# Reordering the query stage of a six-layer transformer kernel: key products half a turn later, folds spread over both halves

## The chip, the cores and the metric

The kernel runs on one core of a Trainium2 chip. A core has five engines with their own instruction streams, which wait for each other on semaphores: TensorE (PE in the rows; its weight loads are PEld), VectorE (DVE), ScalarE (ACT), GpSimd (POOL) and SyncE (SP), which here issues every DMA. The metric is the device time of one execution in microseconds (us); lower is better.

## The reference

The program is six residual layers over x, 16 samples of 64 tokens with 256 channels: a cross attention with low-rank keys, a self attention, a feed-forward layer, a second cross attention, a gated delta-rule layer and a mixture of experts. The change touches the first half of the first one, whose queries are

```
q_hk  = (hidden_q @ Wq.T).reshape(Bv, Sv, H, K)          # H = 16 heads, K = 128
q_big = jnp.einsum('bshk,hkq->bshq', q_hk, w_kc_q)       # q: 192
q_big = _apply_rope(q_big, sin_q, cos_q)
q_r   = jnp.einsum('bshq,hqr->bhsr', q_big, W_qr)
k_r   = jnp.einsum('bld,hdr->bhlr', kv_r, W_kr)
scores = jnp.einsum('bhsr,bhlr->bhsl', q_r, k_r)
```

The kernel folds the weight matrices first (Wq with w_kc_q, W_qr with W_kr), so that a head costs one product of the 1024 normalized tokens with a 256 x 192 matrix, the rotation, and one product with a 192 x 64 matrix.

## The kernel before

The program has four phases; the change lies in `phase1` (lines 154 to 497), the query stage. It works on pairs of heads in eight turns (`u` = 0 to 7, `PAIRS0`), and the 1024 tokens are split into two halves (`f` = 0, 1) of 512. The order of work is written out by hand, for each engine a list of calls in its block:

- **TensorE.** `fold(h)` (L278) multiplies the weights of head h into PSUM bank 0, two matmuls with 192 columns. `fold_pair(u)` (L288) does the small weight products of the pair into bank 1. `queries(u, f)` (L300) multiplies one half of the tokens with the folded weights `cw`: three banks `t` = 0, 1, 2 (2 to 4 for half 0, 5 to 7 for half 1), two matmuls each, which the trace records as 12 instructions of 512 columns. `keys(u, f)` (L313) multiplies the rotated queries `rot` with `mw`, 12 matmuls (24 records) that overwrite the first two banks of that half. `turn(t)` transposes one tile of tokens.
- **ScalarE.** `folded(h)` (L353) moves bank 0 into `cw`, `swap(u, f)` (L363) copies the third bank with its quarters exchanged into `sw` (four instructions), `keep_keys(u, f)` (L373) moves the key products into `tts`.
- **VectorE.** `rope(u, f)` (L430) is the rotation, nine operations of 512 columns; it reads the three banks, `sw` and tables, and leaves `rot`. The additions at L442, L444 and L449 read SBUF alone. `latent` and `butterfly` are side work of the turns 1 to 6, for later layers.
- **GpSimd.** Two multiplications of the weights `ug` by a scale (L405), as soon as their 2 MB have landed, and one of `dn` (L407).
- **SyncE.** `load(h)` (L190) fetches one head's weights: `wk` (384 KB) and `wr` (64 KB), double-buffered, and waits before it until `fold_pair` has released the buffer (`wf`). `store(u, f)` (L197) writes `tts` to DRAM. `ahead(u)` (L214) fetches weights of later layers, among them the 2 MB `ug` in turn 2. Everything goes through one queue in program order.

What each waits for: `queries(u, 0)` for `cw` of both heads (`cs`), `queries(u, f)` from turn 1 on for `keep_keys(u-1, f)` (`ts0`, `ts1`), since the key products lie in its banks; `fold(h)` for ScalarE to have moved the fold before (`cs`); `keys(u, f)` for the rotation (`rope0`, `rope1`). TensorE's loop:

```
for u in range(PAIRS0):
    queries(u, 0)
...
    queries(u, 1)
    if u + 1 < PAIRS0:
        fold(2 * u + 2)
    keys(u, 0)
    if u + 1 < PAIRS0:
        fold(2 * u + 3)
        fold_pair(u + 1)
    keys(u, 1)
```

After the last turn SyncE reads the stored queries back (`load_queries`, L203), once all of half 0 has landed, and only then stores the last half 1; then all engines meet at a barrier.

Of the kernel before, what the change touches and what calls it, by code (L numbers as in the profile page):

```python
# [7 lines left out]
ACT = mybir.ActivationFunctionType  # L8
# [3 lines left out]
B, S, D = 16, 64, 256  # L12
TILES = B * S // P
DC = D // P
L, DCTX = 128, 64
# [138 lines left out]
def phase1(nc, d, sb, semaphores, C, over, X, HT, PS, con, carrier, bn, mv, ve, rstd, hn, kvr, kvT, ctT, TTd, W2, weights, early, b1, q):  # L154
# [4 lines left out]
    with ExitStack() as ctx:  # L159
# [27 lines left out]
        with nc.Block() as block:  # L187
            @block.sync
            def _(sp):
                def load(h):  # L190
                    if h > 1:
                        sp.wait_ge(s["wf"], h // 2)
                    sp.dma_start(wk[:, h % 2, :], d["l0x_k"][h:h + 1, :, :].rearrange("a p n -> (a p) n")).then_inc(s[f"w{h % 2}"], 16)
                    sp.dma_start(wr[64 * (h % 2):64 * (h % 2) + R0, h // 2 % 2, :], d["l0x_r"][h:h + 1, :, :].rearrange("a p n -> (a p) n")).then_inc(s[f"w{h % 2}"], 16)

# [59 lines left out]
                load(3)  # L255
                for u in range(PAIRS0):
                    ahead(u)
                    store(u, 0)
                    if u + 2 < PAIRS0:
                        load(2 * u + 4)  # L260
                        load(2 * u + 5)
                    if u == PAIRS0 - 1:
                        sp.wait_ge(s["ctt"], 16)
                        sp.wait_ge(s["next"], 14 * 16)
                        load_queries()
                    store(u, 1)

            @block.tensor
            def _(pe):
# [16 lines left out]
                    mm.then_inc(s["cf"], 1)  # L286

                def fold_pair(u):  # L288
                    if u > 0:
                        pe.wait_ge(s["ws"], u)  # L290
                    for t in range(3):
                        for r in range(2):
                            rows = slice(64 * r, 64 * r + R0)
                            mm = pe.matmul(PS[rows, 1, t * DCTX:(t + 1) * DCTX], wr[rows, u % 2, t * 64:(t + 1) * 64], wr[rows, u % 2, CQ:RW],
                                           start=True, stop=True)
                    for r in range(2):
                        mm = pe.matmul(PS[64 * r:64 * r + DCTX, 1, D:2 * D], wk[:, r, D + CQ:D + CQ + DCTX],
                                       wk[:, r, D + CQ + DCTX:KW], start=True, stop=True)
                    mm.then_inc(s["wf"], 1)

                def queries(u, f):
                    if f == 0:
                        pe.wait_ge(s["cs"], u * 2 + 2)
                    if u == 0:
                        pe.wait_ge(s["hT"], 4 * f + 4)
                    else:
                        pe.wait_ge(s[f"ts{f}"], u)
                    for t in range(3):
                        for k in range(DC):
                            mm = pe.matmul(PS[:, qbank(f, t), :], cw[:, u % 2, k, t * P:(t + 1) * P],  # L310
                                           HT[:, k, f * 512:(f + 1) * 512], start=(k == 0), stop=(k == DC - 1))
                    mm.then_inc(s[f"q{f}"], 1)
# [19 lines left out]
                for u in range(PAIRS0):  # L332
                    queries(u, 0)
                    if u == 0:
                        for t in range(4, 8):
                            turn(t)
                    queries(u, 1)
                    if u + 1 < PAIRS0:
                        fold(2 * u + 2)
                    keys(u, 0)  # L340
                    if u + 1 < PAIRS0:
                        fold(2 * u + 3)
                        fold_pair(u + 1)
                    keys(u, 1)

            @block.scalar
            def _(a):
# [5 lines left out]
                def folded(h):  # L353
# [1 line left out]
                    a.wait_ge(s["cf"], h + 1)  # L355
                    a.activation(cw[:, u % 2, :, :].rearrange("p k (t r n) -> p k t r n", t=3, r=2)[:, :, :, p, :],
                                 PS[:, 0, 0:DC * CQ].rearrange("p (k t n) -> p k t n", k=DC, t=3), ACT.Copy).then_inc(s["cs"], 1)
                    if p == 1:
                        a.wait_ge(s["wf"], u + 1)
                        a.activation(mw[:, u % 2, :, :], PS[:, 1, 0:3 * DCTX].rearrange("p (t n) -> p t n", t=3), ACT.Copy).then_inc(s["ms"], 1)  # L360
                        a.activation(W2[:, u, :], PS[:, 1, D:2 * D], ACT.Copy).then_inc(s["ws"], 1)

                def swap(u, f):  # L363

# [16 lines left out]
                    keep_hT(t)  # L381
                folded(0)
                folded(1)
                for u in range(PAIRS0):
                    if u == 0:
                        for t in range(4, 8):
                            keep_hT(t)
                    swap(u, 0)
                    swap(u, 1)
                    if u + 1 < PAIRS0:  # L390
                        folded(2 * u + 2)
                    keep_keys(u, 0)
                    if u + 1 < PAIRS0:
                        folded(2 * u + 3)
                    keep_keys(u, 1)

            @block.gpsimd
            def _(g):
# [11 lines left out]
            def _(v):  # L410
# [79 lines left out]
                v.wait_ge(s["cons"], 16)  # L490
                for u in range(PAIRS0):
                    rope(u, 0)
                    rope(u, 1)
                    if 1 <= u <= 6:
                        latent(u - 1)
                    if 4 <= u <= 6:
                        butterfly(u - 4)

# [1954 lines left out]
```

## Time and profile before

| | |
|---|---|
| median of 3 runs | 1542.12 us (1539.15 to 1542.85) |
| the profiled execution | 1550.27 us |
| its span, first to last instruction | 1548.2 us |
| TensorE busy | 1408.3 us (91%) |
| VectorE busy | 1104.5 us (71%) |
| ScalarE, GpSimd busy | 602.0 us, 607.7 us (39% each) |
| the query stage's turns | 17.5 to 174 us of the span |
| in 17.4 to 182 us: TensorE, VectorE, ScalarE busy | 132.0, 111.8, 59.4 us of 164.6 |

The busy time of TensorE counts a matmul from its start to its modelled end, so overlapping ones add up to more than the engine's real occupation; where this text speaks of how long TensorE is taken, it goes by the distance between starts. In a row of the timeline the first number is the start, the second the time to the end of the merged group, and the bracket says how long the engine was idle before and whose result ended that.

### The profile page before, as it was taken

What the parts mean: (1) busy time and instruction counts of PE and PEld (TensorE: products, weight loads), DVE (VectorE), ACT (ScalarE), POOL (GpSimd) and SP (SyncE); (2) the same over time, 40 slices, a digit from 0 to 9 for tenths busy, and PEclk for the clock granted to TensorE, in tenths of its full rate; (3) what the DMA queues carried; (4) which work ended last, traced back from release to release, by engine and by line L of the source; (5) the groups of instructions that cost most, each with busy time, mean ns of one, the idle gap of its engine ahead of it and who ended that gap; (6) DMA issues with size and microseconds to landing.
All of it is one profiled execution on the core that took longest, in us unless ns stands there. A gap on an engine that the chain in (4) does not pass through costs nothing. (4 is left out here: it accounts for less than half of the span.)

```text
span 1548.2 us, 32593 instructions
## 1 busy us (share of the span) xinstructions
PE 1408.3 (91%) x13504; PEld 974.7 (63%) x13504; DVE 1104.5 (71%) x1710; ACT 602.0 (39%) x1012; POOL 607.7 (39%) x935
## 2 busy tenths in 40 slices
PE   6788689999997878999999999999999878999999
PEld 3344368877885445667766666776667665655556
DVE  5768486588557777998898988889999735534443
ACT  3333254345324533554445555445445421111110
POOL 1200143244314646567656657665657610000000
PEclk9999899999998999999999999999999988999999
DMA  8534300110000131121222121222122105000000
GB/s 227 178 89 112 75 1 1 28 28 2 1 1 1 31 78 37 42 58 42 55 52 46 40 58 43 55 51 51 48 44 51 34 18 218 0 1 0 14 1 14
DMA packets 125955, 74.63 MB, mean 48 GB/s; under 512 B 95536, under 2 KB 107056, under 8 KB 124016
## 3 DMA queue, kind: packets, MB, share of 16 engines
q1 hardware_dynamic: 125808, 72.55, 17.9%
q8 instruction: 107, 1.75, 0.5%
q14 instruction: 40, 0.33, 0.1%
HBM read 54.68 MB, written 17.83 MB: 47 GB/s over the span
## 5 line engine op out<-in xcount | busy, mean ns | idle before, releaser
L1877 DVE SCALAR_TENSOR_TENSOR W<-PS,wc,W 128x504 f32<-128x504 f32 x375 | 271.0, 732 | 31.6 <-ACT W L1570 21.9
L1570 ACT ACTIVATE W<-PS,wc 128x512 f32<-128x512 f32 x125 | 85.9, 687 | 154.0 <-PE PS L1273 94.9
L2207 PE MATMUL PS<-HT,wgu 128*128 128x512 f32 x320 | 143.5, 592 | 0.0
L1273 PE MATMUL PS<-HT,wv 128*128 128x512 f32 x252 | 120.2, 608 | 6.8 <-DVE W L1877 6.8
L2341 DVE SCALAR_TENSOR_TENSOR act<-th,PS 128x512 f32<-128x512 f32 x48 | 33.0, 687 | 128.8 <-ACT th L2267 128.8
L1458 PE MATMUL PS<-wo,ogT 128*128 128x256 f32 x512 | 117.2, 388 | 7.6 <-DVE dl L1948 5.1
L1273 PE MATMUL PS<-HT,wkq 128*128 128x512 f32 x248 | 118.1, 620 | 2.9 <-DVE W L1877 2.9
L1296 PE MATMUL PS<-wz,HT 128*128 128x256 f32 x512 | 120.0, 386 | 0.0
L1458 PEld LDWEIGHTS PS<-wo,ogT 128*128 128x128 f32 x512 | 99.3, 195 | 22.2 <-DVE dl L1948 5.3
L2267 ACT ACTIVATE th<-PS 128x512 f32<-128x512 f32 x48 | 28.7, 597 | 206.4 <-PE PS L2207 206.4
L1296 PEld LDWEIGHTS PS<-wz,HT 128*128 128x128 f32 x512 | 94.6, 191 | 17.4 <-issue 4.0
L1777 POOL TENSOR_TENSOR rr<-nm,con 128x8 f32<-128x8 f32 x16 | 31.9, 1994 | 182.7 <-DVE nm L1908 182.7
L1574 ACT ACTIVATE W<-W 128x512 f32<-128x512 f32 x125 | 78.5, 628 | 61.3 <-DVE W L1877 59.7
L2207 PEld LDWEIGHTS PS<-HT,wgu 128*128 128x128 f32 x320 | 60.6, 190 | 60.2 <-issue 58.4
L1808 POOL TENSOR_TENSOR tm<-sy,ti 128x15 f32<-128x15 f32 (+7 forms) x240 | 69.8, 291 | 55.4 <-DMA sy<-a_rows 37.9
L2219 PE MATMUL PS<-wd,act 128*128 128x256 f32 x384 | 89.8, 379 | 0.0
L2219 PEld LDWEIGHTS PS<-wd,act 128*128 128x128 f32 x384 | 72.7, 190 | 26.4 <-issue 18.6
L310 PE MATMUL PS<-HT,cw 128*128 128x512 f32 x192 | 86.7, 607 | 0.5 <-ACT HT L350 0.5
L1273 PEld LDWEIGHTS PS<-HT,wkq 128*128 128x128 f32 x248 | 47.9, 199 | 57.3 <-issue 49.7
L1810 POOL TENSOR_TENSOR ti<-ti,tm 128x15 f32<-128x15 f32 (+7 forms) x240 | 71.6, 298 | 18.8
L1273 PEld LDWEIGHTS PS<-HT,wv 128*128 128x128 f32 x252 | 44.0, 189 | 50.0 <-issue 45.9
L1888 DVE SCALAR_TENSOR_TENSOR yB<-W 128x512 f32<-128x512 f32 x64 | 62.2, 973 | 6.7 <-ACT W L1574 5.4
(277 smaller groups left out, 2938.1 us busy)
## 6 DMA issues: line engine op xcount, KB each, us to landing
a_rows<-AT SPq DMA_DIRECT2D x16, 512.0 KB, 3.1
wk<-in_l0x_k SPq DMA_DIRECT2D x16, 384.0 KB, 3.9
wgu<-in_moe_gu SPq DMA_DIRECT2D x5, 1024.0 KB, 16.4
queries_scratch<-tts SPq DMA_DIRECT2D x32, 128.0 KB, 2.8
wkq<-in_gdn_w SPq DMA_DIRECT2D x16, 256.0 KB, 3.1
wv<-in_gdn_w SPq DMA_DIRECT2D x16, 256.0 KB, 2.9
wz<-in_gdn_w SPq DMA_DIRECT2D x16, 256.0 KB, 2.7
wo<-in_gdn_w SPq DMA_DIRECT2D x16, 256.0 KB, 2.9
```

Source lines behind the costliest of these rows:

```text
L310: mm = pe.matmul(PS[:, qbank(f, t), :], cw[:, u % 2, k, t * P:(t + 1) * P], HT[:, k, f * 512:(f + 1) * 512], start=(k == 0), stop=(k == DC ...
L1273: mm = pe.matmul(PS[:, qbank(h, q), :], w[:, o:o + DK], HT[:, k, f * 512:(f + 1) * 512], start=(k == 0), stop=(k == DC - 1))
L1296: mm = pe.matmul(PS[:, zbank(j, m), w * 256:(w + 1) * 256], HT[:, k, n * P:(n + 1) * P], wz[:, k * 2 * DK:(k + 1) * 2 * DK], start=(k == 0 ...
L1458: mm = pe.matmul(PS[:, wbank(m), w * D:(w + 1) * D], ogT[:, hv, n * P:(n + 1) * P], wo[:, hv, :], start=(hv == 0), stop=(hv == 1))
L1570: a.activation(acc[:, flows(h, q), :], PS[:, qbank(h, q), :], ACT.Copy, scale=wc[:, h % 2, 4 * c + 3:4 * c + 4]).then_inc(s["tap"], 1)
L1574: a.activation(th[:, flows(h, q), :], acc[:, flows(h, q), :], ACT.Tanh, scale=0.5).then_inc(s["th"], 1)
L1808: g.tensor_tensor(t, each(sy[:, c, c + 1:SUB], m), over(ti[:, 0, c, 0:m], n), ALU.mult).then_inc(s["sub"], 1)
L1810: g.tensor_tensor(ti[:, 0, c + 1:SUB, 0:m], ti[:, 0, c + 1:SUB, 0:m], t, ALU.subtract).then_inc(s["sub"], 1)
L1877: v.scalar_tensor_tensor(a0, p0, wc[:, h % 2, 4 * c + 2 - k:4 * c + 3 - k], a0, ALU.mult, ALU.add).then_inc(s["conv"], 1)
L1888: v.scalar_tensor_tensor((yA, yB)[f][:, c, :], th[:, k, :], 1.0, acc[:, k, :], ALU.add, ALU.mult).then_inc(s["y"], 1)
L2207: mm = pe.matmul(PS[:, 2 * (i % 2) + w, :], pack[:, k, w, :], HT[:, k, f * N:(f + 1) * N], start=(k == 0), stop=(k == DC - 1))
L2219: mm = pe.matmul(acc(t)[:, 0:D], act[:, i % RING, t * P:(t + 1) * P], wd[:, m, :], start=(m == 0), stop=(m == MC - 1))
```

## The change

TensorE's loop gets another order, and ScalarE's with it. The two folds of the next pair no longer follow `queries(u, 1)` together: `fold(2u+2)` and `fold_pair(u+1)` come behind `queries(u, 0)`, `fold(2u+3)` behind `queries(u, 1)`. `keys(u, 1)` is done in the next turn, between the two query halves; `keys(u, 0)` stays in its turn, behind `queries(u, 1)` and the fold. The banks inside `queries` are filled in the order 2, 0, 1, and the wait for `keep_keys` comes only before bank 0. `load(h)` also waits for the fold that used the buffer (`cf`), `fold_pair` also for the second weights (`w1`), `store(u, 0)` goes behind the two loads in SyncE's queue, and on VectorE `latent` stands between the two rotations.

```diff
@@ sync @@
                     if h > 1:
                         sp.wait_ge(s["wf"], h // 2)
+                        sp.wait_ge(s["cf"], h - 1)
...
                 for u in range(PAIRS0):
                     ahead(u)
-                    store(u, 0)
                     if u + 2 < PAIRS0:
                         load(2 * u + 4)
                         load(2 * u + 5)
+                    store(u, 0)
@@ tensor @@
                 def fold_pair(u):
+                    pe.wait_ge(s["w1"], u * 32 + 32)
...
                     if u == 0:
                         pe.wait_ge(s["hT"], 4 * f + 4)
-                    else:
-                        pe.wait_ge(s[f"ts{f}"], u)
-                    for t in range(3):
+                    for t in (2, 0, 1):
+                        if u > 0 and t == 0:
+                            pe.wait_ge(s[f"ts{f}"], u)
...
+                    if u + 1 < PAIRS0:
+                        fold(2 * u + 2)
+                        fold_pair(u + 1)
+                    if u > 0:
+                        keys(u - 1, 1)
                     queries(u, 1)
                     if u + 1 < PAIRS0:
-                        fold(2 * u + 2)
+                        fold(2 * u + 3)
                     keys(u, 0)
-                    if u + 1 < PAIRS0:
-                        fold(2 * u + 3)
-                        fold_pair(u + 1)
-                    keys(u, 1)
+                keys(PAIRS0 - 1, 1)
@@ scalar @@
                     swap(u, 0)
+                    if u + 1 < PAIRS0:
+                        folded(2 * u + 2)
+                    if u > 0:
+                        keep_keys(u - 1, 1)
+                    if u + 1 < PAIRS0:
+                        folded_pair(u + 1)
                     swap(u, 1)
                     if u + 1 < PAIRS0:
-                        folded(2 * u + 2)
+                        folded(2 * u + 3)
                     keep_keys(u, 0)
-                    if u + 1 < PAIRS0:
-                        folded(2 * u + 3)
-                    keep_keys(u, 1)
+                keep_keys(PAIRS0 - 1, 1)
@@ vector @@
                     rope(u, 0)
-                    rope(u, 1)
                     if 1 <= u <= 6:
                         latent(u - 1)
+                    rope(u, 1)
```

`folded_pair(u)` is the second half of the old `folded`, the moves of bank 1 into `mw` and `W2`. In the order of instructions TensorE's turn 1 reads before (L310 are the queries, L284 a fold, L294 and L297 the pair's products, L322 the key products):

```order
L310 MATMUL PS<-HT,cw 128x512 x12
L284 MATMUL PS<-wk 128x192 x2
L322 MATMUL PS<-rot,mw 64x256 x12
L284 MATMUL PS<-wk 128x192 x2
L294 MATMUL PS<-wr 64x64 x6
L297 MATMUL PS<-wk 64x256 x2
L322 MATMUL PS<-rot,mw 64x256 x12
```

and in the changed kernel:

```order
L312 MATMUL PS<-HT,cw 128x512 x6
L285 MATMUL PS<-wk 128x192 x2
L296 MATMUL PS<-wr 64x64 x6
L299 MATMUL PS<-wk 64x256 x2
L324 MATMUL PS<-rot,mw 64x256 x12
L312 MATMUL PS<-HT,cw 128x512 x6
L285 MATMUL PS<-wk 128x192 x2
L324 MATMUL PS<-rot,mw 64x256 x12
```

The same instructions stand in the turn; the queries are now cut in two, and each half is followed by a fold and by key products, of which the first (the upper L324) are those of the turn before. In turn 0 there are no such products, and after turn 7 one set is left over.

SyncE's queue around the 2 MB transfer of turn 2 reads before

```order
L223 DMA ug<-in_ffn_ug 128x4096
L200 DMA queries_scratch<-tts 64x4x128 x2
L193 DMA wk<-in_l0x_k 128x768
L194 DMA wr<-in_l0x_r 64x256
```

and in the changed kernel

```order
L201 DMA queries_scratch<-tts 64x4x128 x4
L224 DMA ug<-in_ffn_ug 128x4096
L194 DMA wk<-in_l0x_k 128x768
L195 DMA wr<-in_l0x_r 64x256
```

(`ug`, `wk` and `wr` are weights, `queries_scratch` is the DRAM copy of the queries). The stores of half 0 no longer stand between the 2 MB and the next weights; the first load follows at once.

## Rows read from the trace of the kernel before

**Rows 1.** The page's first line: length of the profiled span

```profile
span 1548.2 us, 32593 instructions
```

**Rows 2.** Waits from 17 to 185 us, longest in total first: us, times, longest

```profile
PE PS L322 <- DVE rot L449: 17.6, 9, 7.3
PE PS L284 <- ACT cw L356: 6.4, 7, 1.0
```

**Rows 3.** Timeline, TensorE, one turn: start us, us, engine, line, op, xcount, [idle before]

```profile
38.24 10.57 PE L310 MATMUL PS<-HT,cw 128*128 128x512 f32 x24
48.65 0.81 PE L284 MATMUL PS<-wk 128*128 128x192 f32 x4
49.45 1.53 PE L322 MATMUL PS<-rot,mw 64*64 64x256 f32 x24
51.89 0.89 PE L284 MATMUL PS<-wk 128*128 128x192 f32 x4 [0.91 <-ACT cw L356]
53.20 0.65 PE L297 MATMUL PS<-wk 128*64 128x256 f32 x4
54.88 1.53 PE L322 MATMUL PS<-rot,mw 64*64 64x256 f32 x24 [1.02 <-DVE rot L449]
56.34 4.13 PE L310 MATMUL PS<-HT,cw 128*128 128x512 f32 x9
```

**Rows 4.** Timeline, ScalarE, the same turn

```profile
43.70 2.38 ACT L370 ACTIVATE sw<-PS 32x512 f32<-32x512 f32 x4 [4.72 <-PE PS L310]
48.84 2.38 ACT L370 ACTIVATE sw<-PS 32x512 f32<-32x512 f32 x4 [2.77 <-PE PS L310]
51.26 0.49 ACT L356 ACTIVATE cw<-PS 128x384 f32<-128x384 f32 x1
51.64 0.59 ACT L377 ACTIVATE tts<-PS 128x512 f32<-128x512 f32 x1
```

**Rows 5.** Timeline, VectorE, the same turn

```profile
43.70 0.69 DVE L437 TENSOR_TENSOR ra<-PS,con 128x512 f32<-128x512 f32 x1 [6.96 <-PE PS L310]
54.74 2.28 DVE L454 TENSOR_TENSOR kvT<-b,con 128x2048 f32<-128x2048 f32 x1
```

**Rows 6.** Timeline around the stall in turn 2, all engines

```profile
58.42 0.60 SPq L223 DMA_DIRECT2D ug<-in_ffn_ug  x1
67.26 9.43 POOL L405 TENSOR_TENSOR ug<-ug,b 128x2048 f32<-128x2048 f32 x2 [52.28 <-DMA ug<-in_ffn_ug]
72.26 4.98 DVE L444 TENSOR_TENSOR rot<-rc,rd 128x512 f32<-128x512 f32 x1
79.22 2.84 PE L322 MATMUL PS<-rot,mw 64*64 64x256 f32 x24 [7.27 <-DVE rot L449]
81.99 3.42 PE L310 MATMUL PS<-HT,cw 128*128 128x512 f32 x5
88.45 1.79 ACT L370 ACTIVATE sw<-PS 32x512 f32<-32x512 f32 x3 [5.73 <-PE PS L310]
```

**Rows 7.** Timeline of turn 0: SyncE's queue, then TensorE between the halves

```profile
19.10 1.63 SPq L194 DMA_DIRECT2D wr<-in_l0x_r  x1
21.40 0.47 SPq L194 DMA_DIRECT2D wr<-in_l0x_r  x1
24.51 0.68 PE L275 MATMUL PS<-con,hn 128*128 128x128 f32 x4 [0.35 <-ACT HT L350]
25.66 1.55 PE L310 MATMUL PS<-HT,cw 128*128 128x512 f32 x3 [0.47 <-ACT HT L350]
```

**Rows 8.** DMA issues from 19 to 20 us, then 21.3 to 21.8: us to landing

```profile
wr<-in_l0x_r SPq DMA_DIRECT2D x1, 64.0 KB, 9.2
wr<-in_l0x_r SPq DMA_DIRECT2D x1, 64.0 KB, 8.2
```

**Rows 9.** Timeline, TensorE, the last key products

```profile
172.02 2.13 PE L322 MATMUL PS<-rot,mw 64*64 64x256 f32 x24 [3.90 <-DVE rot L449]
```

**Rows 10.** Windows, 173 to 174 us: busy by engine, granted clock, DMA share, GB/s

```profile
173.00:174.00 1.00, 1.00 (x12) 0.27 (x4) 0.00 (x0) 0.00 (x0) 0.00 (x0) 0.50 0.42 59
```

More of the change, by code:

```diff
@@ L357, in folded, with folded_pair @@
                                  PS[:, 0, 0:DC * CQ].rearrange("p (k t n) -> p k t n", k=DC, t=3), ACT.Copy).then_inc(s["cs"], 1)
[L358 to L361, printed above, removed]
+                def folded_pair(u):
+                    a.wait_ge(s["wf"], u + 1)
+                    a.activation(mw[:, u % 2, :, :], PS[:, 1, 0:3 * DCTX].rearrange("p (t n) -> p t n", t=3), ACT.Copy).then_inc(s["ms"], 1)
+                    a.activation(W2[:, u, :], PS[:, 1, D:2 * D], ACT.Copy).then_inc(s["ws"], 1)
                 def swap(u, f):
@@ L383, in _ @@
                 folded(1)
+                folded_pair(0)
                 for u in range(PAIRS0):
```

## Prediction

> **What bounds the kernel now.** I read the timeline of the query stage first, engine by engine, since a change of order can only move waits. The rows give one undisturbed turn, turn 1, from 38.24 to 56.34 us, so 18.10 us long [rows 3]. TensorE's own work in it, by distances between starts: 24 query records 10.41 us (48.65 less 38.24), a fold 0.80 (49.45 less 48.65), twice 1.60, a set of key products 1.46 (56.34 less 54.88), twice 2.92, and the pair's products at most 1.16 (from 51.89 + 0.80 to the end of the last at 53.20 + 0.65). That is 16.09 us; the other 2.0 are two gaps, 0.91 us for the fold's bank, which ScalarE moves only after its swap, and 1.02 us for VectorE's last addition [rows 3]. VectorE's two rotations take 11.04 us (54.74 less 43.70) with 2.28 of side work behind them [rows 5]. So TensorE is the bound in a plain turn, with two avoidable gaps.
>
> The waits by engine, the second view, name the same two for the whole stage: 17.6 us for the rotation and 6.4 us for `cw` [rows 2]. But 7.3 of the 17.6 are one wait. The timeline around it: the 2 MB of `ug` are issued at 58.42 and land at 67.26; GpSimd then multiplies for 9.43 us; in that time a VectorE addition of two SBUF tiles lasts 4.98 us, where the whole rotation is 5.52; TensorE idles 7.27 us and goes on at 79.22, and turn 3 starts at 81.99 instead of 74.4 [rows 6]. And it goes on slowly: the key products take 2.77 us (81.99 less 79.22) instead of 1.46, the first query half 6.46 us to its swap (88.45 less 81.99) instead of 5.46 (43.70 less 38.24) [rows 3, 4, 6]. That is TensorE at its lower level, 1.2 GHz; the tail shows the same after 3.90 us idle, 24 products in 2.13 us and a granted clock of 0.50 [rows 9, 10].
>
> **The plain turn after the change.** No instruction is added or removed on any engine in a turn. TensorE's chain, from the start of `queries(u, 0)`: first half 5.27 us (43.70 less 0.19 less 38.24; the swap starts 0.19 after the next TensorE work, 48.84 against 48.65), fold 0.80, pair 1.16, key products of the turn before 1.46, second half 5.14. Call this point F, 13.83 us in. Fold and key products take 2.26 more. The rotation of half 0 started at 5.46 and lasts 5.52, so it is done at 11.0, well before F + 0.80: the gap of 1.02 us is gone. The other gap only moves. The next queries need both halves of `cw`, and ScalarE moves the second behind its swap: before, the swap started at 48.84, the move at 51.26 and TensorE at 51.89, which is F + 3.24 [rows 3, 4]. So TensorE waits 3.24 - 2.26 = 0.98 us. The turn is 13.83 + 3.24 = 17.07; cutting the queries in two may show one weight load that was hidden, nothing to 0.2 us, and I take 17.1. **Each plain turn gains 1.0 us.**
>
> The other order of banks costs nothing and avoids a loss: ScalarE ends `keep_keys` at F + 0.19 + 2.42 + 0.38 + 0.59 = F + 3.6 [rows 4], and bank 0 is now wanted at F + 3.24 plus four records, 1.7 us; wanted first, it would have been 0.4 late. `keys(u, 1)` waits for a rotation that started at F + 0.19 and ended at F + 5.7; it is wanted at F + 10.5. Even with `latent` between the rotations (2.28 us, done at 13.3, half 1 ready at 14.0) VectorE keeps up.
>
> **Turn by turn**, against the profiled execution:
>
> - Turns 1, 3, 4, 5, 6: 5 x 1.0 = 5.0 us gained.
> - Turn 2: it lasted 81.99 - 56.34 = 25.65 us. In the new order `ug` is issued behind the store of `keys(1, 1)`, about 10.7 us into turn 2, and lands 8.84 later, 2.5 us into turn 3. GpSimd holds 2.5 to 11.9. The rotation of turn 2's half 1 ends at 2.4; that of turn 3's half 0 starts at 5.46, meets its first addition at 7.9, waits to 11.9 and ends at 15.0. Its key products are wanted at 14.6, and the 0.98 us wait follows anyway. The next rotation runs 17.3 to 22.8 and is wanted at 24.3. So this stall is hidden: 25.65 - 17.1 = 8.55 gained, and 1.0 for the slow clock in turn 3. What it costs without that cover is between 0 and what it cost before, 6.25 us and the clock.
> - Turn 0: here it gets worse. `fold(2)` and `fold_pair(1)` now stand before `queries(0, 1)`, which ran at 25.66. Their weights are behind the context tensors in the queue: issued 19.10 and 21.40, landing after 9.2 and 8.2 us, at 28.3 and 29.6 [rows 7, 8]. TensorE is free at 25.2 (24.51 + 0.68) and idles 3.1 us; the half starts at 29.6 + 1.16 = 30.8, 5.1 later. From there to turn 1 it was 12.58 us (38.24 less 25.66) and is 5.14 + 3.24 = 8.38, as one set of key products is left out and both gaps are less. Net 0.9 us lost.
> - The clock in turn 0: 3.1 us idle lies between the 1.02 us, after which the turn ran on at full rate, and 3.90 us, after which it did not [rows 3, 9]. Bounds 0 and 2.3 us (1.3 + 1.0 from the stall above); I take 1.1, the middle, as the row at 3.90 is the nearer.
> - Turn 7: one more set of key products before the last query half, 1.46 + 0.1: 1.6 lost. Behind the last half both programs are the same: the last swap, `keep_keys`, the read back.
> - Weights: `load(8)` now follows the 2 MB at once. At 2 MB in 8.84 us its 448 KB land 1.9 us behind them, 21.5 us into turn 2, wanted at 22.4; `load(9)` at about 23.4, wanted at 23.2. Between 0 and 1 us late, I take 0.3. The other moves in SyncE's queue have some microseconds of room: a store is awaited only a turn later.
>
> Sum: 5.0 + 8.55 + 1.0 - 0.9 - 1.1 - 1.6 - 0.3 = **10.7 us less**. The profiled execution took 1550.3 us with a span of 1548.2 [rows 1], 8 us above the median of the runs shown; the rows of the stage are waits set by order, which the other runs have too, so I take the difference off the median: 1542.1 - 10.7 = **1531.4 us**. Its own range is 1529 to 1535.
>
> **What the skill adds.** On the idle time in turn 0 the Trainium skill (TensorE: Matmul & The Clock Gate, section "Why this matters for your kernels") warns of idle gaps between bursts of matmuls, since the clock falls to its lower level in one. By it the full 2.3 us would be due and the result 1532.6 instead of 1531.4; the row at 3.90 us agrees with it, the rows show nothing at 3.1.
>
> The Trainium skill (SBUF — State Buffer, section "SBUF: two separate sides") has GpSimd and a VectorE operation with two SBUF inputs exclude each other for a whole instruction, whoever starts first. The 4.98 us addition agrees; where the 2 MB land in the new order decides who is held, which is the first rival.
>
> **Rivals.**
>
> 1. **The stall of turn 2 returns in turn 3.** GpSimd's 9.43 us still fall on the rotations. If the 2 MB land 3 or 4 us later than I have them (the weights behind them share the DMA engines), both multiplications can catch an addition each, and the key products wait. For it: 15.0 against 14.6 has no room. Against: every rotation now has some 4 us before it is wanted. Whole, it gives back 6.25 + 2.3: 1540; half of it 1535.5. Chance 0.08 and 0.10.
> 2. **Slower: the second weights arrive late in every turn.** `load(2u+5)` now waits for `fold(2u+3)`, is issued about 14.7 us into the turn, and `fold_pair` wants it at 17.1 + 6.1, 8.5 us later; before, both loads could go at 53.85 and were wanted from 66.75 on, 12.9 later (56.34 + 10.41) [rows 3]. It decides from a landing time of 8.5 us. In turn 0 such loads took 9.2 and 8.2 us [rows 8]. For a loss of over 0.3% each of six turns would have to wait 2.6 us, a landing of 11 us: with the idle time the clock would fall too, and the result would be 1548. Against it: the 9.2 us were behind over 3 MB. Chance 0.04.
> 3. **It goes better:** turn 0's weights land before they are wanted and no slow clock follows, or the 0.98 us wait is shorter: 10.7 + 1.1 + 0.3 and up to 3 more, 1527. Chance 0.08.
> 4. **The change does not do what it says:** the gap of 1.02 only joins the other one, as TensorE waits for `cw` longer (the move then comes behind something else in ScalarE's order). Turns stay at 18.1, the rest holds: 5 + 1 less gained, 1537.4. Chance 0.06; a small remainder, 0.04, I leave for no change.
>
> **The numbers.** The forecast has 0.60. A measurement can tell about 0.3%, 4.6 us, from no change. Faster by more than that, below 1537.5: the forecast, half of rival 1, rivals 3 and 4, 0.60 + 0.10 + 0.08 + 0.06 = 0.84, and 0.02 of the edge of rival 1. Within: the rest of it and the remainder, 0.10. Slower: 0.04. Range: from rival 3 to rival 1's whole price, 1527 to 1539, which leaves out rival 2, half of the whole of rival 1 and the ends.
>
> **What would show it.** In the profile after, a plain turn of 17.1 us with one wait of 0.9 to 1.0 us before `queries(u, 0)`, for `cw`, and none for the rotation until the last turn; no wait of over 1.5 us in turns 2 and 3, though a VectorE addition of 4 us; in turn 0 a wait of 3 us before the third fold and `queries(0, 1)` at about 30.8; turn 7 starting near 143 us (40.2 + 6 x 17.1 + 0.3). Wrong would be: a wait for the rotation in turn 3, turns above 17.5 us, or a wait for weights in every turn.

## The result and the profile after

The changed kernel takes 1535.47 us, median of 14 runs (1530.4 to 1539.67), beside 1542.59 us for the kernel before (14 runs, 1538.02 to 1547.27). The two medians differ by 7.1 us; the ratio is 0.9948, with a 95% interval of 0.9935 to 0.9960, which makes it 8.0 us faster, between 6.2 and 10.0. The forecast was 1531.4 with a range of 1527 to 1539, and faster; its own narrower range, 1529 to 1535, is missed by 0.5 us. The profiled execution took 1532.53 us. Of all the executions told of below, one ran in a slower state (1853.50 us at a mean granted clock of 0.745 instead of 0.97, the kernel with turn 0 in the old order) and is in no ratio.

The page's first lines, length of the span and TensorE's busy time:

```profile
span 1530.5 us, 32607 instructions
PE 1409.0 (92%) x13504; PEld 972.7 (64%) x13504; DVE 1097.3 (72%) x1710; ACT 601.7 (39%) x1012; POOL 608.7 (40%) x935
```

The span is 17.7 us below that of before [rows 1], much more than the runs differ. So the span can't be the measure; the stage that was changed has to be read by itself. Its waits, the view that answers to [rows 2] (us in total, times, longest):

```profile
PE PS L312 <- ACT cw L360: 6.0, 7, 0.9
PE PS L324 <- DVE rot L459: 4.5, 2, 3.9
PE PS L285 <- DMA wr<-in_l0x_r: 3.4, 1, 3.4
```

The wait for the rotation was 17.6 us and is 4.5, 3.9 of it the last key products, where it stood before as well [rows 9]. The wait for ScalarE's `cw` is still there, 6.0 for 6.4 us, now ahead of the queries. New is a wait of 3.4 us for weights.

TensorE's timeline of turn 1, the answer to [rows 3] (start, us, line, [idle before]; L312 are the queries, L285 a fold, L296 and L299 the pair's products, L324 the key products):

```profile
42.09 5.42 PE L312 MATMUL PS<-HT,cw 128*128 128x512 f32 x12 [0.89 <-ACT cw L360]
47.34 0.81 PE L285 MATMUL PS<-wk 128*128 128x192 f32 x4
48.09 0.56 PE L296 MATMUL PS<-wr 64*64 64x64 f32 x12
48.58 0.65 PE L299 MATMUL PS<-wk 128*64 128x256 f32 x4
49.17 1.53 PE L324 MATMUL PS<-rot,mw 64*64 64x256 f32 x24
50.62 5.42 PE L312 MATMUL PS<-HT,cw 128*128 128x512 f32 x12
55.88 0.81 PE L285 MATMUL PS<-wk 128*128 128x192 f32 x4
56.62 1.53 PE L324 MATMUL PS<-rot,mw 64*64 64x256 f32 x24
59.03 5.42 PE L312 MATMUL PS<-HT,cw 128*128 128x512 f32 x12 [0.89 <-ACT cw L360]
```

The turn lasts 59.03 - 42.09 = 16.94 us, where it was 18.10. One gap is left, 0.89 us for `cw`; the key products at 49.17 (those of turn 0) and at 56.62 start without one.

Turn 0, the same view, from the last token transposes to the fold behind the query half:

```profile
24.20 0.68 PE L276 MATMUL PS<-con,hn 128*128 128x128 f32 x4 [0.35 <-ACT HT L354]
28.30 1.17 PE L285 MATMUL PS<-wk 128*128 128x192 f32 x4 [3.41 <-DMA wr<-in_l0x_r]
29.88 0.91 PE L296 MATMUL PS<-wr 64*64 64x64 f32 x12 [0.41 <-DMA wr<-in_l0x_r]
31.77 7.33 PE L312 MATMUL PS<-HT,cw 128*128 128x512 f32 x12
38.93 0.81 PE L285 MATMUL PS<-wk 128*128 128x192 f32 x4
```

and the busy times and granted clock (third number from the right) in one microsecond of it:

```profile
29.00:30.00 1.00, 0.59 (x4) 0.12 (x4) 0.74 (x2) 0.49 (x1) 0.00 (x0) 0.50 1.06 379
```

TensorE is free at 24.9, waits 3.4 us for the first weights and 0.4 us for the second, and starts the half at 31.77. By then it runs at its lower level, 1.2 GHz: the half takes 38.93 - 31.77 = 7.16 us instead of the 5.26 of the same half in turn 1 (55.88 - 50.62).

The 2 MB of `ug` and what they release, answering to [rows 6]: SyncE's queue, GpSimd, VectorE's longest addition, TensorE's key products of turn 3 and the next queries.

```profile
69.60 0.61 SPq L224 DMA_DIRECT2D ug<-in_ffn_ug  x1
78.37 9.12 POOL L415 TENSOR_TENSOR ug<-ug,b 128x2048 f32<-128x2048 f32 x2 [63.37 <-DMA ug<-in_ffn_ug]
83.83 4.21 DVE L452 TENSOR_TENSOR rot<-ra,rb 128x512 f32<-128x512 f32 x1
90.72 1.53 PE L324 MATMUL PS<-rot,mw 64*64 64x256 f32 x24
92.92 5.42 PE L312 MATMUL PS<-HT,cw 128*128 128x512 f32 x12 [0.68 <-ACT cw L360]
```

GpSimd still holds an addition, now for 4.21 us, and the only trace of it on TensorE is that the key products start 0.2 us late and the wait behind them is 0.68 instead of 0.89 us. Turn 3 lasts 92.92 - 75.98 = 16.94 us like its neighbours.

The end of the stage: turn 6's first fold, turn 7's start and the first product of phase 2.

```profile
132.25 0.92 PE L285 MATMUL PS<-wk 128*128 128x192 f32 x4
144.16 5.42 PE L312 MATMUL PS<-HT,cw 128*128 128x512 f32 x12 [0.89 <-ACT cw L360]
172.30 5.32 PE L588 MATMUL PS<-dn,con 128*128 128x512 f32 x8 [7.10 <-POOL vb L917]
```

Turn 7 starts at 144.16 and phase 2 at 172.30; in the trace of before these two are at 155.38 and 181.87. The change brings them forward by 11.2 and 9.6 us. Turn 6 is 0.4 us longer than the others (144.16 - 126.81 = 17.35).

Behind the stage nothing was changed, yet phase 3, from its first product to that of phase 4, lasts 789.9 us in the profile of before and 782.7 in that of after. Little of that can be the change: in ten other profiles of the changed kernel and its variants, and in two of variants of the kernel before, it lies anywhere from 780.1 to 786.5 us, and the 8.0 us of the repeated executions leave no room for 7.2 besides the stage's 9.6. The 17.7 us of the two spans are 9.6 us of the stage, 1.1 of phase 2 and 7.2 of phase 3, where one execution happened to be the slowest of all and the other below the middle (phase 4 is 0.2 us longer).

### The profile page after: what moved, and what is told of

It reads as the page before. It is cut to its first block and busy times, and to the rows that moved or that the text cites. A ratio compares the mean times of both kernels' runs of the same rounds, so it can differ in the third digit from the quotient of the medians.

```text
span 1530.5 us, 32607 instructions
## 1 busy us (share of the span) xinstructions
PE 1409.0 (92%) x13504; PEld 972.7 (64%) x13504; DVE 1097.3 (72%) x1710; ACT 601.7 (39%) x1012; POOL 608.7 (40%) x935
## 3 DMA queue, kind: packets, MB, share of 16 engines
q8 instruction: 107, 1.75, 0.5%
## 5 line engine op out<-in xcount | busy, mean ns | idle before, releaser
L312 PE MATMUL PS<-HT,cw 128*128 128x512 f32 x192 | 89.1, 615 | 6.0 <-ACT cw L360 6.0
L312 PEld LDWEIGHTS PS<-HT,cw 128*128 128x128 f32 x192 | 36.1, 196 | 53.1 <-issue 43.4
```

## The experiments

All starts below are from TensorE's timeline. "Turn 1" and "turn 7" are the starts of `queries(1, 0)` and `queries(7, 0)`.

| kernel | turn 1 | a plain turn | turn 3 | turn 7 | ratio to before |
|---|---|---|---|---|---|
| before | 38.24 | 18.10 | 19.1 | 155.38 | 1 |
| changed | 42.09 | 16.94 | 16.94 | 144.16 | 0.9948 (0.9935 to 0.9960) |
| changed, second profile | 41.73 | 16.94 | 16.94 | 143.37 | 0.9942 (0.9921 to 0.9963) |
| wait filled | 39.54 | 16.94 | 16.95 | 142.16 | one run |
| old bank order | 42.00 | 18.28 | 18.27 | 151.67 | one run |
| before, no `ug` scaling | 38.07 | 18.10 | 18.10 | 146.65 | one run |
| `latent` in its old place | 39.99 | 16.94 | 21.92 | 147.92 | one run |
| turn 0 in the old order | 35.88 | 16.94 | 16.93 | 138.28 | 0.9916 (0.9883 to 0.9949) |
| context later | 35.41 | 16.94 | 16.94 | 137.36 | 0.9907 (0.9873 to 0.9941) |
| both folds early | 40.69 | 15.98 | 23.53 | 145.35 | 0.9959 (0.9935 to 0.9983) |
| folds early, context later | 37.30 | 15.98 | 17.54 | 135.91 | 0.9922 (0.9892 to 0.9953) |
| before, GpSimd in pieces | 38.76 | 18.10 | 19.50 | 152.53 | 0.9973 (0.9951 to 0.9994) |
| `latent` old, GpSimd in pieces | 40.51 | 16.94 | 16.94 | 142.48 | one run |
| all together | 35.39 | 15.98 | 16.23 | 131.72 | 0.9879 (0.9850 to 0.9908) |

My theory was that the gain is waits taken out by order: 1 us a turn, and the stall of turn 2 hidden, against a loss in turn 0. The rivals: that the stall comes back in turn 3, and that weights arrive late.

### Turn 0: filling the wait

```diff
@@ tensor, behind the transposes of turn 0 @@
+                    if u == 0:
+                        for r in range(4):
+                            pe.matmul(PS[:, 7, :], cw[:, 0, 0, 2 * P:3 * P], HT[:, 0, 0:512], start=True, stop=True)
```

> The changed kernel with four extra products of 512 columns (eight records, 3.4 us) into the unused bank 7 in turn 0, between the token transposes and fold(2), where TensorE waits 3.4 us for weights. Theory 1 (the wait costs its length and then, through TensorE's lower clock, a second time): queries(0, 1) starts at 30.8 to 31.0 instead of 31.77 and lasts 5.2 us to the next fold instead of 7.16, so turn 1 starts near 39.1 instead of 42.09, a gain of 3.0 us. Rival (the slow products come from the DMA traffic or from the first use of the weights, not from idle time): the half still lasts about 7.2 us and turn 1 starts at 42 or later.

The two query halves that follow, `queries(0, 1)` and `queries(1, 0)`:

```profile
31.13 5.42 PE L312 MATMUL PS<-HT,cw 128*128 128x512 f32 x12
39.54 5.42 PE L312 MATMUL PS<-HT,cw 128*128 128x512 f32 x12 [0.89 <-ACT cw L363]
```

and the same microsecond as above, busy times and granted clock:

```profile
29.00:30.00 1.00, 0.42 (x3) 0.12 (x1) 0.54 (x1) 0.49 (x1) 0.00 (x0) 1.00 1.02 366
```

The half starts at 31.13 and turn 1 comes 8.41 us later, the full-rate distance; in the changed kernel it is 10.32 (42.09 less 31.77). Turn 1 starts 2.55 us earlier than in the profile of the changed kernel, most of the expected 3.0, and the granted clock is 1.00 where it was 0.50. The products computed here are thrown away, so the wait itself stays and what goes is its clock.

How much that clock costs differs from one execution to the next. The kernel with `latent` in its old place (below) has the same turn 0 as the changed one, with nothing filled in. It waits 3.56 us, its granted clock falls to 0.50 as well, but is back at full as the half begins:

```profile
31.58 5.42 PE L312 MATMUL PS<-HT,cw 128*128 128x512 f32 x12
```

Its turn 1 starts at 39.99, only 0.45 us behind that of the filled wait; in the second profile of the changed kernel it is 41.73, so 2.19 us. So the fall of the clock is shown, and its price in turn 0 was anything from 0.45 to 2.55 us in these executions.

### Turn 0: two ways to avoid the wait

```diff
@@ tensor and scalar, turn 0 only @@
+                    if u == 0:
+                        queries(u, 1)
                     if u + 1 < PAIRS0:
                         fold(2 * u + 2)
                         fold_pair(u + 1)
```

> The changed kernel with turn 0 alone in the old order: queries(0, 1) straight behind the transposes, then fold(2), fold_pair(1), fold(3) and keys(0, 0). Theory 1: queries(0, 1) starts at 25.4, nothing waits for weights, fold(3) waits about 1 us for ScalarE, turn 1 starts near 36 instead of 42.1 us; stage 6 us shorter, ratio to before 0.4% below that of the changed kernel (0.9948). Rival (the weights bound turn 0 in any order, as they land at 28.3 and 29.6): gain of 2 us or less.

```diff
@@ sync @@
+                load(2)
+                load(3)
                 sp.dma_start(cx[:, :, :], d["ctx"]).then_inc(s["ctx"], 16)
                 sp.dma_start(cr[:, :, :], d["ctx_rolled"]).then_inc(s["ctx"], 16)
                 sp.dma_start(ctT[:, :, :, :].rearrange("p t b s -> p (t b) s"), d["ctxT"][:, :, 0:S]).then_inc(s["ctt"], 16)
-                load(2)
-                load(3)
```

> The changed kernel with three context transfers (ctx, ctx_rolled, ctT: 1.25 MB) behind load(3) in SyncE's queue. Theory 1 (the weights are late only because they stand behind the context tensors): load(2) and load(3) land by 25, queries(0, 1) starts near 27.2, turn 1 near 35.6 instead of 42.1; ratio to before about 0.991. Rival (landing is set by the 448 KB themselves and SyncE's issue after fold_pair(0)): they land at 27 or later and the gain is under 2 us.

The second one's halves, `queries(0, 1)` and `queries(1, 0)`:

```profile
27.00 5.42 PE L312 MATMUL PS<-HT,cw 128*128 128x512 f32 x12
35.41 5.42 PE L312 MATMUL PS<-HT,cw 128*128 128x512 f32 x12 [0.88 <-ACT cw L360]
```

27.00 and 35.41 were expected at 27.2 and 35.6. The other edit puts turn 1 at 35.88 (expected 36). Both take 6.2 to 6.7 us out of turn 0, and their ratios, 0.9916 and 0.9907, agree with it (0.0032 and 0.0041 below that of the changed kernel, 4.9 and 6.3 us of 1542). So the place of the weights in the queue is the cause of turn 0's loss, and either end of it can be mended. The two ratios' intervals overlap with that of the changed kernel; that both are faster than it rests on the starts in the traces more than on the times.

### The order of the banks

```diff
-                    for t in (2, 0, 1):
+                    for t in (0, 1, 2):
                         if u > 0 and t == 0:
                             pe.wait_ge(s[f"ts{f}"], u)
```

> The changed kernel with the banks filled 0, 1, 2 again and the wait for keep_keys ahead of bank 0, which is now ahead of all. Theory 1 (the key products come just before the queries that overwrite their banks, so ScalarE's move of them is exposed): queries(u, 0) waits 0.45 us longer than the 0.89 for cw, and queries(u, 1) 0.85 us where it waits for nothing now; a turn lasts 18.2 us instead of 16.94, and turn 7 starts near 152 instead of 144.2. Rival (ScalarE is quick enough and the bank order is worth nothing): turns of 16.9 to 17.1 us.

The two halves of turn 1:

```profile
42.00 5.39 PE L312 MATMUL PS<-HT,cw 128*128 128x512 f32 x12 [1.47 <-ACT tts L382]
51.29 5.42 PE L312 MATMUL PS<-HT,cw 128*128 128x512 f32 x12 [0.72 <-ACT tts L382]
```

Both halves now wait for `tts`, 1.47 us (0.58 more than the wait for `cw`) and 0.72 us. A turn takes 18.28 us and turn 7 starts at 151.67, as expected (18.2 and 152). Without the new bank order the new order of key products would have been worth nothing in a plain turn: 18.28 against 18.10.

### The stall of turn 2

```diff
@@ gpsimd, in the kernel before @@
-                    g.tensor_tensor(ug[:, k, :], ug[:, k, :], wsu[:, :], ALU.mult).then_inc(s["ugd"], 1)
+                    g.tensor_tensor(ug[:, k, 0:8], ug[:, k, 0:8], wsu[:, 0:8], ALU.mult).then_inc(s["ugd"], 1)
```

> The kernel before, with GpSimd's two multiplications of ug cut from 2048 to 8 columns (most of the scaling of ug is left out). Theory 1 (the 7.27 us wait of turn 2 is GpSimd holding VectorE's additions): no addition over 0.7 us in turn 2, turns 2 and 3 of 18.1 us each, 8.5 us of the stage gone. Rival (the 2 MB transfer itself or the side work on VectorE holds turn 2): a wait of 5 us or more stays in turn 2.

This kernel leaves out the scaling of all but 8 columns of `ug`; it serves to take GpSimd's work away.

The queries of turns 3 and 4:

```profile
74.26 10.57 PE L310 MATMUL PS<-HT,cw 128*128 128x512 f32 x24
92.36 10.57 PE L310 MATMUL PS<-HT,cw 128*128 128x512 f32 x24
```

Turn 2 lasts 18.09 us (74.26 less its start, 56.17), turn 3 18.10, and turn 7 starts at 146.65, 8.7 us before that of the kernel before. The 2 MB are still fetched. The stall was GpSimd's, and it was worth what the prediction took it for: 7.6 us in turn 2, of which 1.3 are its slow key products, and 1.0 us of slow queries in turn 3.

### The place of `latent`

```diff
                     rope(u, 0)
+                    rope(u, 1)
                     if 1 <= u <= 6:
                         latent(u - 1)
-                    rope(u, 1)
```

> The changed kernel with latent behind both rotations again. Theory 1 (the place of latent is worth nothing, since every rotation is ready 4 us before it is wanted): turns of 16.94 us as in the changed kernel, turn 3 at most 0.3 us different, turn 7 starting at 144.2 give or take 0.5. Rival (latent behind rope(u, 1) delays rope(u+1, 0) past its use): turns 1 to 3, which have 2.28 us of it, at least 0.5 us longer.

Here both theories missed what came. GpSimd, two VectorE operations of turn 2 (its last addition, then `latent`) and the key products of turn 3:

```profile
75.78 9.44 POOL L415 TENSOR_TENSOR ug<-ug,b 128x2048 f32<-128x2048 f32 x2 [60.71 <-DMA ug<-in_ffn_ug]
75.84 5.00 DVE L459 TENSOR_TENSOR rot<-re,rf 128x512 f32<-128x512 f32 x1
80.76 6.61 DVE L466 TENSOR_TENSOR b<-b,con 128x2048 f32<-128x2048 f32 x1
93.03 2.84 PE L324 MATMUL PS<-rot,mw 64*64 64x256 f32 x24 [4.56 <-DVE rot L459]
```

The 2 MB land 1.90 us into turn 3 (75.78 less 73.88). GpSimd holds the last addition of turn 2 for 5.00 us, then `latent(1)`, which reads SBUF alone, for 6.61; the rotation of turn 3 starts at 87.29 instead of 79.3, and its key products wait 4.56 us. Turn 3 lasts 21.92 us, 5.0 more than in the changed kernel, while turns 1 and 2, with as much side work, stay at 16.94. So my theory that `latent`'s place is worth nothing fell; and the rival, that `latent` itself is too long there, did too. The landing of the 2 MB isn't what differs: with `latent` between the rotations they land 0.7 to 2.4 us into turn 3 in six profiles (1.89 with the context later), and in none of the six do that turn's key products wait for the rotation.

The same kernel with GpSimd's instructions cut tells whether it is their length:

```diff
@@ gpsimd @@
-                    g.tensor_tensor(ug[:, k, :], ug[:, k, :], wsu[:, :], ALU.mult).then_inc(s["ugd"], 1)
+                    for j in range(4):
+                        n = slice(j * 512, (j + 1) * 512)
+                        g.tensor_tensor(ug[:, k, n], ug[:, k, n], wsu[:, n], ALU.mult).then_inc(s["ugd"], 1)
```

(The multiplication of `dn` is cut up too, and the wait for `ugd` counts the pieces; so in the other runs with pieces.)

> The changed kernel with latent behind both rotations (as in the run of that name, which had a wait of 4.56 us for the rotation in turn 3), and GpSimd's multiplications in pieces of 512 columns. Theory 1 (that wait came from GpSimd's long instructions alone): turn 3 lasts 16.9 to 17.3 us, no wait for the rotation over 0.5 us. Rival (latent in its old place delays the next rotation by itself): turn 3 still has a wait of 3 us or more.

The wait for the rotation in the whole stage but its end (total, times, longest), and `latent(1)`:

```profile
PE PS L324 <- DVE rot L462: 0.9, 1, 0.9
76.97 3.35 DVE L469 TENSOR_TENSOR b<-b,con 128x2048 f32<-128x2048 f32 x1
```

`latent(1)` takes 3.35 us for 6.61, turn 3 is back at 16.94, and its key products wait for nothing. The one wait for a rotation, 0.9 us, stands in turn 7 (0.55 us there in the changed kernel). Theory 1 holds: the cost came from the length of GpSimd's instructions.

### The stall in pieces, without the new order

```diff
@@ gpsimd, in the kernel before @@
-                    g.tensor_tensor(ug[:, k, :], ug[:, k, :], wsu[:, :], ALU.mult).then_inc(s["ugd"], 1)
+                    for j in range(4):
+                        n = slice(j * 512, (j + 1) * 512)
+                        g.tensor_tensor(ug[:, k, n], ug[:, k, n], wsu[:, n], ALU.mult).then_inc(s["ugd"], 1)
```

> The kernel before, with GpSimd's two multiplications of ug cut into eight of 512 columns each (and that of dn into eight). Theory 1 (a VectorE addition is held by the GpSimd instruction under way, 4.7 us, not by the amount of work): each addition is held by 1.2 us at most, the wait of turn 2 falls from 7.27 to under 4 us, turn 2 lasts 20 us or less instead of 25.65, the stage is 6 to 8 us shorter, ratio about 0.996. Rival (GpSimd takes the port again before VectorE gets it, so the additions still wait for the whole 9.4 us): turn 2 stays at 24 to 26 us, ratio 1.00.

GpSimd, two of VectorE's additions in turn 2, the key products behind them:

```profile
67.48 14.07 POOL L407 TENSOR_TENSOR ug<-ug,b 128x512 f32<-128x512 f32 x8 [52.42 <-DMA ug<-in_ffn_ug]
70.83 1.75 DVE L447 TENSOR_TENSOR rot<-rc,rd 128x512 f32<-128x512 f32 x1
74.29 1.63 DVE L452 TENSOR_TENSOR rot<-re,rf 128x512 f32<-128x512 f32 x1
75.98 2.84 PE L322 MATMUL PS<-rot,mw 64*64 64x256 f32 x24 [3.51 <-DVE rot L452]
```

Each of the two additions is held by about 1 us (1.75 and 1.63 for 0.68) and the product between them by 0.5, as expected, and the wait falls from 7.27 to 3.51. But several are held in a row, GpSimd takes 14.07 us for the same work instead of 9.43, and TensorE still falls to its lower level: turn 2 lasts 21.90 us and turn 3 19.50. Turn 7 starts 2.9 us earlier (3.4 us in turns 1 to 6, as turn 1 starts 0.5 us late in this execution), not 6 to 8, and the ratio 0.9973 agrees. Theory 1 had the hold and the wait right and the lengths wrong: the whole of GpSimd's work isn't waited for, but cutting it up gives back less than half of the 8.6 us that went with its work, where the new order hides all of them.

### The remaining wait, and all together

```diff
@@ tensor; scalar likewise @@
+                    if u + 1 < PAIRS0:
+                        fold(2 * u + 3)
                     queries(u, 1)
-                    if u + 1 < PAIRS0:
-                        fold(2 * u + 3)
                     keys(u, 0)
```

> The changed kernel with fold(2u+3) ahead of queries(u, 1), so that ScalarE moves it before the swap. Theory 1 (the remaining 0.89 us wait of each turn is the swap standing before the cw move): turns of 16.1 to 16.2 us instead of 16.94, turn 7 starting 5 us earlier, near 139; ratio 0.3% lower than the changed kernel's. Rival (the wait turns into one for keep_keys at bank 0): turns of 16.5 us or more.

A plain turn is 15.98 us, even below what I expected, and the 0.89 us wait is gone. But turn 3 takes 23.53. GpSimd, two operations of the rotation `rope(2, 1)` and its key products in turn 3:

```profile
75.40 9.41 POOL L414 TENSOR_TENSOR ug<-ug,b 128x2048 f32<-128x2048 f32 x2 [60.36 <-DMA ug<-in_ffn_ug]
75.52 4.93 DVE L456 TENSOR_TENSOR rf<-sw,con 128x512 f32<-128x512 f32 x1
80.49 4.87 DVE L458 TENSOR_TENSOR rot<-re,rf 128x512 f32<-128x512 f32 x1
85.41 2.84 PE L324 MATMUL PS<-rot,mw 64*64 64x256 f32 x24 [5.60 <-DVE rot L458]
```

In a shorter turn the 2 MB land while two SBUF operations of one rotation are still to come, and each multiplication catches one: 4.93 and 4.87 us. (`rf<-sw,con`, the product with `sw`, has two SBUF inputs like the three additions.) The key products wait 5.60 us and go on at the lower clock (2.84 us for 1.53). This is the first rival of the prediction, nearly whole, by a shift of a microsecond: 7.55 us are given back of the 8.55 it was priced at, turn 7 starts at 145.35 instead of the expected 139, and the version is no faster than the changed kernel (0.9959).

> Both of the last two edits together. Theory 1: they add, stage 11 us shorter than in the changed kernel, ratio to before about 0.988. Rival (VectorE becomes the bound: 11.04 us of rotations, side work, and GpSimd's hold in turn 3): less than 8 us, with waits for the rotation in turns 3 to 6.

With both edits, the second fold of turn 0 and the first fold of turn 6:

```profile
28.18 1.34 PE L285 MATMUL PS<-wk 128*128 128x192 f32 x4 [1.76 <-ACT cw L360]
124.79 0.92 PE L285 MATMUL PS<-wk 128*128 128x192 f32 x4 [0.60 <-DMA wr<-in_l0x_r]
```

Turn 7 starts at 135.91, 8.2 us earlier than in the changed kernel where I expected 11. Three things take the rest: `fold(3)` waits 1.76 us for ScalarE in turn 0 and the lower clock follows, so turn 1 starts 1.9 us later than with the context transfers moved alone; additions are caught in turn 3 (17.54 us); and in turn 6 (17.14 us) the weights are 0.6 us late, behind the ten transfers of `ahead(5)`, 1.1 MB. The plain turns aren't bound by VectorE, so neither theory has it whole.

The last version has an answer to each of the three:

```diff
@@ sync @@
                 for u in range(PAIRS0):
-                    ahead(u)
                     if u + 2 < PAIRS0:
                         load(2 * u + 4)
                         load(2 * u + 5)
+                    ahead(u)
                     store(u, 0)
@@ tensor; scalar likewise @@
+                    if 0 < u < PAIRS0 - 1:
+                        fold(2 * u + 3)
                     queries(u, 1)
-                    if u + 1 < PAIRS0:
-                        fold(2 * u + 3)
+                    if u == 0:
+                        fold(3)
                     keys(u, 0)
```

besides the context transfers behind `load(3)` and GpSimd's work in pieces, as above.

> The changed kernel with fold(2u+3) ahead of queries(u, 1) in turns 1 to 6, three context transfers behind load(3), the loads ahead of ahead(u), and GpSimd's multiplications in pieces. Theory 1: turn 1 starts at 35.4, turns of 16.0 us with no wait over 0.5 us, turn 7 at 131.5 instead of 144.2; ratio to before 0.986, faster than every other version. Rival (VectorE or the weights bound the shorter turns): turns of 16.5 us and more, ratio 0.990 or more.

The first query halves of turns 1, 2 and 3:

```profile
35.39 5.42 PE L312 MATMUL PS<-HT,cw 128*128 128x512 f32 x12 [0.88 <-ACT cw L362]
51.37 5.42 PE L312 MATMUL PS<-HT,cw 128*128 128x512 f32 x12
67.36 5.42 PE L312 MATMUL PS<-HT,cw 128*128 128x512 f32 x12
```

15.98 and 15.99 us a turn, 16.23 and 16.16 in turns 3 and 4, on which GpSimd's work falls, and turn 7 at 131.72 (expected 131.5). The ratio is 0.9879 (0.9850 to 0.9908): 18.7 us faster than the kernel before, and faster than the changed kernel beyond both intervals; from the kernel with the context later (0.9907) the times alone don't separate it. It gains a bit less than the 0.986 of the expectation; the stage has the gain (phase 2 starts at 160.3 against 181.9).

### The changed kernel once more

> The changed kernel once more, for a second profile and more runs. Theory 1 (the stage's gain of 9.6 us is fixed by the order, and what differs between runs lies in turn 0's clock and behind the stage): turn 7 starts at 142.1 or 144.2, turns 1 to 6 as before to 0.1 us, with no wait for the rotation in turn 3; ratio 0.993 to 0.996. Rival (in part of the executions the 2 MB land a little earlier and the stall comes back, as it did with latent in its old place): turn 3 has a wait of 3 us or more.

GpSimd, the last addition of `rope(2, 1)`, the key products of turn 3:

```profile
77.40 9.45 POOL L415 TENSOR_TENSOR ug<-ug,b 128x2048 f32<-128x2048 f32 x2 [62.39 <-DMA ug<-in_ffn_ug]
77.58 4.88 DVE L459 TENSOR_TENSOR rot<-re,rf 128x512 f32<-128x512 f32 x1
90.14 1.53 PE L324 MATMUL PS<-rot,mw 64*64 64x256 f32 x24
```

Turns 1 to 5 are the same to 0.02 us and turn 0 is 0.36 us shorter for its clock. Turn 6 is 16.94 us here, without the 0.4 us that the weights cost it in the first profile, so turn 7 starts at 143.37, at neither of the two expected times, and phase 2 at 171.50, 10.4 us earlier than in the kernel before. In this execution the 2 MB land 1.79 us into turn 3 instead of 2.39, early enough to catch the last addition of turn 2 for 4.88 us as well. The key products of turn 3 follow their fold without a wait all the same, since `latent(1)` is already done. The held addition ends at 82.46 and its own key products are wanted at 82.7: they start on time, with 0.2 us to spare. The first addition of turn 3 is then held for 2.63 us and has room. So the stall stays hidden at either landing, but by little; the version with both folds early, whose turns are 1 us shorter, is past that point.

## Why the prediction was right

**Plain turns: right, 0.16 us better each.** 16.94 us for 17.1, 1.16 gained for 1.0. The pair's products were put at their upper bound of 1.16 us (they take 1.08, 48.09 to 49.17), and the cut of the queries shows no extra weight load. The wait for `cw` moved ahead of the queries as worked out, 0.89 us for 0.98.

**Bank order: right in kind, too small in size.** The text put the avoided loss at 0.4 us, for half 0 alone. Measured it is 0.58 and 0.72, 1.34 us a turn with what follows, more than the whole 1.16 us gained in a turn. The step that was missing is half 1, whose key products stand immediately before the queries that overwrite their banks.

**Turn 2: right.** 25.65 - 16.95 = 8.7 us for 8.55, and in turn 3 the slow clock of 1.0 is gone (2.16 in all). The run without the scaling shows that the cause was the one named. The working behind it, GpSimd from 2.5 to 11.9 us into turn 3, came out at 2.4 to 11.5. What the prediction did not see is why it holds: it took `latent` between the rotations as a burden that VectorE can bear. With `latent` in its old place turn 3 is 5.0 us longer, so that move carries over half of the turn 2 gain.

**Turn 0: the step that was mis-sized.** The working gave 0.9 us for the late weights and 1.1 for the clock, 2.0; turn 1 starts 3.85 us later. The filled wait splits it: 1.3 us for the weights and 2.55 for the clock in this execution, above even the 2.3 taken as the bound. The bound came from a stall after which key products ran first; here a fold, the pair's products and most of a query half ran at 1.2 GHz. By the Trainium skill (TensorE: Matmul & The Clock Gate, section "Why this matters for your kernels") the clock falls when the engine idles between bursts; the traces agree, it fell in every profile with a wait of 3.4 us or more there. Taking the middle of the bounds was a choice against the nearer row. But that row was one execution too: the same 3.90 us of idle time ahead of the last key products is followed, in eleven profiles, by 24 products in anything from 1.53 us (full rate, granted clock 1.00, in the kernel with turn 0 in the old order) to 2.84. With a price between 0.45 and 2.55 us in turn 0, 1.1 was inside what the executions show and missed what this one did. A single row couldn't settle this term.

**Turn 7: right**, 1.65 us for 1.6 (172.30 less 144.16, against 181.87 less 155.38).

**Weights: right in size, wrong in place.** Turns 2 and 3, where 0.3 us was put, show nothing. It is turn 6, behind `ahead(5)`, that has 0.4 us, none in the second profile, and up to 1.0 in the runs with the wait filled and with `latent` in its old place (17.91 and 17.97 us). The slower rival, late weights in every turn, did not come: in turns 1 to 5 no fold waits for a weight.

Sum by the trace: 15.1 us in turns 1 to 6 (1.16 + 8.70 + 2.16 + 1.16 + 1.15 + 0.74), less 3.85 and 1.65, is 9.6 us for the 10.7 of the forecast. Part of this is errors that cancel: turns 1 to 6 gave 0.8 us more than the 14.25 of the forecast, turns 0 and 7 cost 1.9 more than its 3.6. The runs show 8.0 (6.2 to 10.0), and 0.9942 in the second set, 9.0 us. 9.6 is inside both intervals, and the 10.7 itself only in the second (5.7 to 12.2). That the unchanged phases give something back on average is not excluded, and phase 3's spread of 780 to 790 us between profiles is too wide to tell; the 1.6 us between 9.6 and 8.0 stay open.

## What to carry to other kernels

When a reordering is judged by its plain turns, look up where the rare long instructions of other engines land in the new order: an edit that shortened the plain turns by 1 us each gave all of it back, since two operations of one rotation then fell under GpSimd's two instructions, and the move of a side job ahead of the last rotation was what made room for it. Before moving work forward, check when its data land in the first turn, too; a wait of 3.4 us there cost up to 2.5 us more in clock. And where results are written over their inputs' banks, start the next products in the bank that is free.

## What the runs showed of the hardware

- A GpSimd multiplication of 4.7 us held each VectorE operation with two SBUF inputs that started under it until it ended (2.63 to 5.00 us for 0.68, less where the multiplication was further on), and did not slow those with one input in PSUM (0.67 to 0.69 us). Cut into pieces the two alternate, and GpSimd's total grows from 9.4 to 14.1 us.
- After waits of 3.4 to 4.0 us in turn 0 TensorE was at 1.2 GHz (granted clock 0.50) in five of five profiles, but how long it stayed there differed: the query half behind the wait took 5.26, 6.53, 6.79 and 7.16 us in four profiles of three kernels whose turn 0 is the same, the last two of one program. Ahead of the last key products the same 3.90 us of idle time was followed by the full clock in one profile of eleven, and by anything down to half of it in the others. Shorter waits in turn 0, of 2.44 and 1.76 us (`latent` old with GpSimd in pieces; folds early with the context later), were followed by a granted clock of 0.50 too.
- SyncE's issue of a weight transfer took 1.49 us with the context transfers ahead of it and 0.34 us with three of them (1.25 MB) moved behind it (both issued at 17.56 us).
